# A decoder layer over 32 batches on one core: moments of LayerNorm in groups, bias rows by a TensorE product, h as 32-bit words, two buffers of probabilities

## What is computed

```
x = x + SelfAttention(LayerNorm(x) * g + b)      16 heads of 8; a learned relative bias on the scores
x = x + CrossAttention(LayerNorm(x), ctx, mask)  16 heads of 8; masked keys get -1e9
x = x + W_down(silu(W_gate(y)) * W_up(y)),  y = LayerNorm(x)
        ternary weights, activations quantised to 8 bits per row, inner width 512
```

## Time and profile before

| | |
|---|---|
| runs | 461.76, 458.22 and 462.43 us, median 461.76 |
| span of the profiled execution | 457.5 us |
| busy share | PE 87%, DVE 84%, ACT 79%, POOL 72% |
| end of the first batch (L1027) | 93.32 us |
| 27th batch | 399.85 us |

### The profile page before, as it was taken

How to read it: one execution, slowest core, us unless ns; L and a number is a source line. 1 busy time by engine, 2 the same in 40 slices (tenths; PEclk the granted TensorE clock), 3 DMA queues, 4 the chain that set the end, 5 groups by cost and what they waited for, 6 DMA issues and landing times. The chain is left out here.

```text
span 457.5 us, 18022 instructions
## 1 busy us (share of the span) xinstructions
PE 398.0 (87%) x5405; PEld 311.5 (68%) x5436; DVE 385.7 (84%) x1920; ACT 359.9 (79%) x962; POOL 329.2 (72%) x917
## 2 busy tenths in 40 slices
PE   3267879999999999999999999999999999877762
PEld 2245657777777777777877777778877777654430
DVE  4645467999999999999999999999999999888532
ACT  2214758899999999999999999999999998865542
POOL 6834667888888888888888888888888765654120
PEclk9998999999999999999999999999999999998655
DMA  6654577756666766676657675676567662422100
GB/s 190 162 146 100 140 188 184 173 149 172 173 159 160 191 163 168 150 195 172 170 148 196 175 175 153 164 181 170 152 158 189 165 164 80 101 78 77 30 6 13
DMA packets 100181, 67.27 MB, mean 147 GB/s; under 512 B 73269, under 2 KB 90421, under 8 KB 100085
## 3 DMA queue, kind: packets, MB, share of 16 engines
q1 hardware_dynamic: 98209, 64.08, 54.7%
q10 hardware_dynamic: 1876, 2.03, 1.5%
HBM read 46.08 MB, written 19.07 MB: 142 GB/s over the span
## 5 line engine op out<-in xcount | busy, mean ns | idle before, releaser
L895 DVE CUSTOM_DVE_ANT_0 biased<-bank,mask_bias 128x128 bf16<-128x128 f32 x512 | 112.8, 285 | 4.0 <-PE bank L1128 3.9
L900 DVE TENSOR_REDUCE neg_max_S<-bank 128x4 f32<-128x512 f32 x128 | 85.4, 675 | 21.1 <-PE bank L1128 20.4
L599 ACT ACTIVATE probs_S<-bank 128x512 f32<-128x512 f32 x128 | 72.7, 597 | 11.0 <-PE bank L1148 11.0
L599 ACT ACTIVATE probs_X<-bank 128x512 f32<-128x512 f32 x128 | 72.5, 590 | 7.0 <-PE bank L1148 6.4
L1128 PE MATMUL bank<-stack_k_S,stack_q_S 120*128 120x128 bf16 x512 | 50.5, 223 | 11.7 <-DMA stack_k_S<-scratch_S 11.0
L1148 PEld LDWEIGHTS bank<-stack_q_X,stack_k_X 74*128 74x128 bf16 x512 | 41.1, 100 | 16.6 <-issue 2.1
L1128 PEld LDWEIGHTS bank<-stack_k_S,stack_q_S 120*128 120x128 bf16 x512 | 38.6, 102 | 20.1 <-issue 11.9
L1148 PE MATMUL bank<-stack_q_X,stack_k_X 74*128 74x128 bf16 x512 | 51.4, 224 | 0.0
L1145 PE MATMUL bank<-ident_bf,mask_bias 128*128 128x512 bf16 x128 | 50.6, 396 | 0.0
L1128 PE MATMUL bank<-stack_k_X,stack_q_X 72*128 72x128 bf16 x512 | 45.3, 221 | 2.9 <-DMA stack_k_X<-scratch_X 1.7
L1166 PE MATMUL bank<-probs_X,v_aug_X 128*32 128x128 f32 x1024 | 42.4, 285 | 0.0
(11 more groups left out here) (165 smaller groups left out, 1178.6 us busy)
## 6 DMA issues: line engine op xcount, KB each, us to landing
stack_q_S<-scratch_S SPq DMA_DIRECT2D x32, 288.0 KB
stack_k_S<-scratch_S SPq DMA_DIRECT2D x32, 288.0 KB
stack_q_X<-scratch_X SPq DMA_DIRECT2D x32, 288.0 KB
stack_k_X<-scratch_X SPq DMA_DIRECT2D x32, 288.0 KB
scratch_S<-qk_parts_S SPq DMA_DIRECT2D x32, 192.0 KB, 2.7
scratch_X<-qk_parts_X SPq DMA_DIRECT2D x32, 192.0 KB, 2.7
scratch_S<-qk_parts_S SPq DMA_DIRECT2D x32, 64.0 KB, 1.7
ctxT<-ctx SPq DMA_DIRECT2D x8, 256.0 KB, 4.7
```

The lines of the kernel that those rows point to most:

```text
L599: act.activation(probs[a][:, c, :], bank_b[c % 2][:, :], ACT.Exp).then_inc(sems["exp_" + a], 1)
L895: last = dve.tensor_tensor_reduce(biased[:, c, hh, :], quarter(bank_a[c % 2], hh), mask_bias[:, b % 2, :], -1.0, -2.0 * BIG, ALU.add, ALU.min,
L900: dve.tensor_reduce(neg_max[a][:, first_head(c):first_head(c) + 2 * HC - 1:2], bank_a[c % 2][:, :].rearrange("i (h j) -> i h j", h=HC), AX ...
```

## The change

The order of the parts in the lists stays, but there are now three lists: `fill` (S alone), `step` and `drain` (X and F). A step has two counters: S works on s, X and F on x, with s = x + LEAD. Parts are written for all due batches (`st.due`), and bank reuse is kept by `take(bank, readers)` in place of the tuples.

- LayerNorm moments of S are made in groups (1, 3, then 4 batches at a time) at the start of DVE's step, one group a step, so that all are done in the first eight steps; POOL's three operations on them follow at the end of its step, between `max_hi` and `max_lo` of S.
- The loads of x stand first in SP's step.
- The bias rows are no longer added by POOL. They are split into three bf16 rows, and `project_out` adds them with a second product. The residual no longer waits for POOL.
- hT is copied as 128x256 32-bit words with no arithmetic; the offset of the rounding is taken out by a fifth product in `down`. hT and the down weights are f16.
- `probs` has two buffers: the exponential of batch b waits for the products of batch b - 2.
- The constants' places move: in the early steps the ternary weights now stand before the maxima c2 and c3 of S.

The core of the diff:

```diff
-STEPS = [(t, t) for t in range(-1, B + 10)]
+LEAD, TAIL, LAGS = 3, 3, 12
+MOMENTS = (0, 1, 4, 8, 12, 16, 20, 24, 28, 32)
...
+        def run(begun, fill, step, drain):
+            for s in range(-1, LEAD):
+                fill(Step(s, None, begun))
+            for x in range(B + TAIL - LEAD):
+                step(Step(x + LEAD, x, begun))
+            for x in range(B + TAIL - LEAD, B + TAIL + LAGS):
+                drain(Step(x + LEAD, x, begun))
...
@@ SP @@
+            def load_x(st, lag):
+                for g in st.due("S", lag, "load_x", n=B // GROUP - 2):
+                    batches = slice(X_FIRST[2] + g * GROUP, X_FIRST[2] + (g + 1) * GROUP)
+                    sp.dma_start(x_all[:, batches, :], xs[:, batches, :]).then_inc(sems[f"x_loaded{g}"], 16)
+            def fill(st):
+                load_x(st, -2)
+                parts_again("S", st, 0)
+                parts_out("S", st, 0)
...
+                stack_in("S", st, 0)
+                load_c(st, -1)
+                max_in("S", st, 1)
@@ POOL @@
-                add_shift("S", st, 0)
-                add_shift("X", st, 5)
@@ ACT @@
-                    act.wait_ge(sems["av_" + a], done(b - 1, CH, c + 1))
-                act.activation(probs[a][:, c, :], bank_b[c % 2][:, :], ACT.Exp).then_inc(sems["exp_" + a], 1)
+                    if b >= 2:
+                        act.wait_ge(sems["av_" + a], done(b - 2, CH, c + 1))
+                    act.activation(probs[a][:, b % 2, c, :], bank_b[c % 2][:, :], ACT.Exp).then_inc(sems["exp_" + a], 1)
...
-                act.activation(hT[:].rearrange("p c s -> p (c s)"), bank_t[:, 0:256].bitcast(F16), ACT.Identity,
-                               bias=minus_round16[:, 0:1]).then_inc(sems["hT"], 1)
+                    copy(hT[:].rearrange("p c s -> p (c s)").bitcast(F32), bank_t[:, 0:256]).then_inc(sems["hT"], 1)
@@ DVE @@
+            def ln_group(st, lag):
+                for g in st.due("S", lag, "ln_group", n=len(MOMENTS) - 1):
+                    lo, hi = MOMENTS[g:g + 2]
...
+                    for b in range(lo, hi):
...
+                        dve.bn_stats(stats_s[:, b - lo, :], x_all[:, b, :]).then_inc(sems["stats_S"], 1)
+                    for b in range(lo, hi):
+                        dve.wait_ge(sems["stats_S"], b + 1)
+                        dve.bn_aggr(mv_s[:, b, :], stats_s[:, b - lo, :]).then_inc(sems["mv_S"], 1)
+            def fill(st):
+                ln_group(st, -2)
+                if st.at(0):
+                    weight_sums()
...
+                ternary_weights(st, 1)
+                row_max("S", st, 1, 2)
+                row_max("S", st, 1, 3)
@@ PE @@
-                project_qkv("S", st, 0, ("v_X", 4), ("h", 8), ("v_S", 1))
-                project_qkv("X", st, 3, ("h", 7), ("v_S", 0), ("v_X", 4))
+                project_qkv("S", st, -1)
+                project_qkv("X", st, 0)
...
-                pe.matmul(quarter(bank_s, 2), oT[a][:], w_o[a][:], start=True, stop=True)\
+                    pe.matmul(quarter(bank_s, 2), oT[a][:], w_o[a][:], start=True, stop=False)
+                    pe.matmul(quarter(bank_s, 2), ones_bf[:], shift_rows3[:, "SX".index(a), :], start=False, stop=True)\
...
+                    last = pe.matmul(bank_t[:, 256:384], minus_offset[:], w_down_sum[:], start=False, stop=True)
```

More of the change, by code:

```diff
@@ new lines, in store @@
+            def store(st, lag):
+                for b in st.due("F", lag, "store"):
+                    if b < B - GROUP and b % GROUP != GROUP - 1:
+                        continue
+                    n = GROUP if b < B - GROUP else 1
+                    batches = slice(b + 1 - n, b + 1)
+                    sp.wait_ge(sems["res_F"], done(b))
+                    sp.dma_start(out[batches].rearrange("b s d -> s b d"), x_all[:, batches, :])\
+                        .then_inc(sems["out_stored"], 16)
@@ L370, in _ @@
             n = 0
+            begun = {}
             def const(instruction):
@@ L760, in _ @@
+            run(begun, fill, step, drain)
         @block.vector
@@ L1334, in _, with scores_a @@
-            run(step)
+            def scores_a(a, st, lag, c):
+                for b in st.due(a, lag, "scores_a", c):
+                    bank, rows = bank_a[c % 2], slice(0, A_ROWS[a])
+                    take(f"a{c % 2}", ("max_" + a, done(b, CH, c + 1)))
+                    if c == 0:
+                        if a == "S" and b == 0:
+                            pe.wait_ge(sems["stack_ready0"], 16 * STACK_LOADS)
+                        if a == "S" and b == 1:
+                            pe.wait_ge(sems["stack_ready1"], 16 * 2 * (STACKS - 1))
+                        pe.wait_ge(sems[f"stack_in_{a}{b % STACKS}"], loaded(b, 16 * 2))
+                    masked = a == "X" and c not in BIASED
+                    if masked:
+                        pe.wait_ge(sems["mask_bias"], done(b))
+                        pe.matmul(bank[:, :], ident_bf[:], mask_bias[:, b % 2, :].unsqueeze(1).to_broadcast([S, HC, S]),
+                                  start=True, stop=False)
+                    for hh in range(HC):
+                        last = pe.matmul(bank[:, part_of_bank(hh)], stack_q[a][rows, b % STACKS, head(c, hh)],
+                                         stack_k[a][rows, b % STACKS, head(c, hh)], start=not masked,
+                                         stop=not masked or hh == HC - 1)
+                    last.then_inc(sems["score_a_" + a], 1)
@@ new lines, in o_transposed @@
+            def o_transposed(a, st, lag):
+                for b in st.due(a, lag, "o_transposed"):
+                    if a == "S" and b == 0:
+                        pe.wait_ge(sems["ffn_const"], MEAN_W)
+                    pe.wait_ge(sems["o_raw_" + a], done(b))
+                    take("t", ("o_norm_" + a, done(b)))
+                    for half in range(2):
+                        last = pe.transpose(quarter(bank_t, half), o_raw[a][:, half, :], ident[:])
+                    last.then_inc(sems["o_ps_" + a], 1)
```

1605 lines of the change are left out of this document (803 added, 802 removed).

## The result

The changed kernel is slower by 4.5%: 479.51 us median of four runs (477.54 to 481.26) against 459.99 (455.19 to 462.43) on the same chips, ratio 1.0449, 95% interval 1.0373 to 1.0525. The forecast was 469 with a range to 477; the side was right, the size was not. The profiled span is 475.7 instead of 457.5, 18.2 more where 7.1 were forecast.

The account below looks back on a forecast made before the run. No engine was full on average: a 93 us start, 26 full steps of 11.79 us, five lighter ones. Terms 10.0 + 3.0 + 3.0 - 7.0 - 1.9 = +7.1 on 461.76 gave 469.0 us, range 459.5 to 477.

Parts of the forecast that it names:

- A: Start: one more step of S alone, since S runs one batch further ahead of X and F; +10.0 us.
- B: Start, SP's queue: loads of x and ctx ahead of the parts of batch 0 delay them; +3.0 us, 2.0 to 5.5.
- C: Start: DVE and PE work moved ahead of the scores, POOL's group operations costing nothing; +3.0 us, from 0 to 6.
- D: Full steps: removed work outweighs added products; -0.28 us a step, -7.0 over 25 steps, from 0 to -12.3.
- E: End: one full interval becomes one without S, and six without S get lighter; -1.9 us, from 0 to -2.4.
- C's own sign: Early steps: DVE's maxima c2, c3 end late, with PE waiting for them and no longer for stack_k.
- The other half of C: Start, PE: abs_sum product ahead puts the transpose of batch 1 at about 17, 3.0 late; +1.6 us.
- the term of hT: Full steps: ACT's faster hT copy saves 0.31 us, of which PE's waits give back 0.17 a step, 0.11 to 0.23.
- The 0.12 behind the residual of S: Full steps, DVE: removing mv_S between the residual of S and stats_X saves 0.12 us a step.
- ACT and the waits set the step: Rival, full steps: the whole 0.49 us a step comes back and the start costs less; 460.1 us, chance 0.15.
- PE becomes the bound: Rival, full steps: three added products cost 0.24 us each step and nothing comes back; 484 us, chance 0.08.
- B and C are hidden: Rival, start: late loads and maxima vanish in the wait for stack_k; 463.9 us, chance 0.25.

Follow-up runs that it names:

- e15: Kernel before the change with X and F one step further behind S, nothing else: median 469.24 us, ratio 1.0193 to the kernel before.
- e1: Changed kernel with S two steps ahead instead of three: median 474.78 us, ratio 1.0282 to the kernel before.
- e13: Changed kernel with early DVE and POOL work where engines wait, loads behind stack_in, relative-bias rows as before: 467.83 us, ratio 1.0184 to the kernel before.
- e14: e13 with S two steps ahead instead of three: median 462.63 us, ratio 1.0074 to the kernel before.
- e2: Changed kernel with moment groups and ternary weights behind DVE's residual of S, POOL's group operations behind max_lo: 493.52 us, ratio 1.0683 to the kernel before.
- e16: Kernel before the change with ACT's issue of the relative-bias rows one step later, nothing else: 463.63 us, ratio 1.0070 to the kernel before.
- e11: Changed kernel with ACT's relative-bias rows issued one step earlier and POOL's group operations behind rest and part3: 475.61 us, one run.
- e12: e11 with the loads of x and ctx behind stack_in as well: median 473.79 us, ratio 1.0261 to the kernel before.
- e7: Changed kernel without the three added products per step (two for bias rows, one for the offset): 481.31 us, one run.
- e8: Changed kernel with hT copied as 128x512 f16 elements again, no bias tile: 483.68 us, one run.
- e3: Changed kernel with loads of x and ctx behind stack_in of S and one and two steps later: 481.35 us, ratio 1.0429 to the kernel before.
- e5: Changed kernel with POOL's three group operations behind max_lo, rest and part3 of the next step: 478.87 us, ratio 1.0427 to the kernel before.
- e6: Changed kernel with the ternary weights behind the residual of S on DVE: 477.87 us, ratio 1.0410 to the kernel before.
- e10: Changed kernel with ACT's relative-bias rows of stack_k issued one step earlier, as before the change: 480.63 us, one run.
- e17: Changed kernel with six unused PE products ahead of max_transposed of S for batches 1 to 7: 477.56 us, three more runs 485.61 to 488.60.
- e18: e12 with six unused PE products ahead of max_transposed of S for batches 1 to 7: 482.12 us, ratio 1.0435 to the kernel before.

## Why the prediction was wrong

**Where the 11.1 us went.** The start came out at +22.7 where A, B and C made +16.0, and the full steps and the end at -4.5 where D and E made -8.9.

**A, the additional step: right in kind, its exact price in part luck.** 10.0 forecast; 10.3 when added alone to the kernel before (e15), 8.4 when taken from the changed kernel (e1), 7.2 when taken from e13. In e15 the moments of the first X come only 6.1 later (mv_X at 49.12, before 43.01); the other 4.2 arise behind them, in X and F, which A held unchanged. The +22.7 of the start are 11.7 for the places (e13), 7.2 for the step (e14), and 3.8 that stay open.

**C failed, in the step about its cover.** I wrote that max_lo and the second scores stand "behind the first ones in PE's order, and so behind the wait for stack_k: nothing". The order of the parts on PE is another: the transpose of the maxima of one batch stands ahead of the first scores of the next. What is late in c2, c3, max_hi or max_lo thus holds the next scores at once, and their own wait for stack_k ends meanwhile: 1.45 and more before, none after. PE waits 9.1 us ahead of this transpose between 30 and 110, and 3.6 more in the wait with no releaser named. Price: the places together, with the loads and the missed move, are worth 11.7 us of the first batch (e13), where B and C made 6. The order would have shown it, had I read it from max_transposed on and not from the scores. C's own sign came: PE waits for the maxima and no longer for stack_k. That it is the place and not the amount is shown by e13, with the same work; e2 shows that a move meant to help can cost more. How the 11.7 divide among DVE, POOL, the loads and the rows is not shown, since single moves hid one another. The other half of C came nearly as forecast: the transpose of batch 1 at 16.66 (17), its parts issued at 23.70 (23.4), its copies at 28.33, 2.5 late where I took 1.6.

**C, the missed move.** The relative-bias rows on ACT were issued 7.3 us later, and nowhere in the prediction. Added alone to the kernel before, 5.1 late, they cost 0.7% (e16).

**B: right in price, hidden in place.** Issue and landing cost 4.0 us at the copies and 3.0 at the first scores (e11 against e12, one profile each), and 3.0 was forecast. But in the changed kernel POOL and the bias rows held the first scores as long, so moving the loads alone gave nothing. The Trainium skill, "DMA: Bandwidth & Descriptors", section "Queues, rings and completion order", has each DMA engine consume descriptors in ring order; taken alone, this put B at the upper end of my estimate, 5.5 us for all of the 1 MB. The runs show 2.6 us of later issue in SP's queue and 1.4 of later landing, 4.0, between the two ends of 2.0 and 5.5. The loads were issued 1 to 3 us ahead of the parts and had that time to move, so the rule is neither shown nor refuted by this.

**D failed in the term of hT, and its total was too high.** The step gained 0.09, where 0.28 were forecast. The 0.12 behind the residual of S is seen (0.33 became 0.21) and brought 0.08, the difference of e1 to the changed kernel; it needs the lead as well as the removal (e1, e15). The products cost 0.09 (e7), forecast 0.08. What else was removed brought 0.10: e1 has it and the products, and its step is 0.01 below that of before. Of that 0.10 hT has no part, as far as e8 shows, whose copy is 0.22 of the 0.31 slower with no effect; its 0.17 is the term that failed. I had misread the row behind it. Of the 3.4 us that PE sat idle before the down product only 1.6 are put down to hT, and these are two waits in the last part of the program, as the list of what PE waits for before the change shows from 385 to 457:

```profile
PE bank L1278 <- ACT hT L659: 1.6, 2, 0.8
```

From 150 to 350 the same list holds no wait for hT, and none for xn_X; PE waits there once, 0.2 us for stack_k_X. So in the full steps only the weight loads waited, PE itself had nothing to get back, and it was busy for 98% of the time from 200 to 305, before and after. The rest of the 0.10 would be xn_X (0.07 forecast) and what I had left out, such as yT (277 instead of 368 ns); I did not separate them. The weight loads did wait for hT, and hardly do now; they wait for probs_S instead. Over 25 steps the profiles give -2.8 instead of -7.0; 25 times the 0.09 of the step is 2.3, and the averages scatter by more than the rest.

**E: right in number, not tested.** -1.75 against -1.9, but the last six intervals take between 62.1 and 67.2 us in the profiles of e2, e3, e5, e6, e10 to e13, e17 and e18, where nothing of this part was changed, so one pair says little.

**The rivals.** "ACT and the waits set the step" needed at least 0.35 a step and is out, with 0.09. "PE becomes the bound" came nearest in time (484), by another mechanism: it wanted longer full steps, and they became shorter. "B and C are hidden" was wrong: the wait that was to hide them was the thing replaced.

**Open.** e14 has no additional step and all early work in places where an engine waits, and its moments of X come no later than before (mv_X at 42.31, before 43.01), yet its first batch is 3.8 later. This lies in the stage of X, where groups still stand on DVE and POOL, and I did not separate it. How much the lower clock adds is open too. None of the versions is faster than the kernel before; the best, e14, is 0.7% over it.

## What to carry to other kernels

A cover is read from the order of the engine that waits: look which instruction stands ahead of the one that is to hide the lateness, and follow the late value to it. Work that is "off the path" because it is needed much later still delays what is queued behind it on its engine; put it where that engine waits for another one, and read that place from the timeline. Look then at what stands behind the new place, too. Where a list is run with other step numbers, compare the time of every one-time DMA issue, on every queue. And a wait of 0.1 us is worth nothing until it is shown that the loop closes through it. Ask for the stretch of full steps alone, and for the product apart from its weight load; an edit that makes the waited-for operation slower again then tells at once.

## What the runs showed of the hardware

The power of POOL took 1.04 us for 128x4 elements and 0.575 for 128x1, while the two tensor_scalar operations beside it stayed at 0.20 and 0.24: grouping four batches nearly halves its total (8.9 us instead of 18.4), but makes the single one twice as long for whoever waits behind it. The copy of the same 128 KB on ACT took 687 ns as f16 with a bias tile, 598 as f16 without one, and 383 as 32-bit words. PE's granted clock from 40 to 100 us, one profile each, was 0.97 in the kernel before, e13 and e14, 0.86 in the changed kernel, and 0.77 in e12: it differed with where the early work stood.
